# Slots ahead of the gates, table angles in VectorE's gaps, and table doublings with both parts in one instruction

## What is computed

```python
xn = layernorm(x)
# state space part: a long convolution per channel, whose kernel K has 1024 taps
V  = exp(dtA[:, :, None] * l[None, None, :])        # complex, 128 heads x 64 states x 1024 lags
K  = 2 * real(einsum('hn,hnl->hl', Ct, V))
y  = irfft(rfft(xn) * rfft(K))[:1024]
# experts part: 8 experts, each row goes to its best 2
gate_logits = einsum('bsd,ed->bse', xn, Wg)
gating = softmax over the two largest logits
out = sum over those two: gating * (silu(xn W1) * (xn W2)) W3
x = x + layernorm(...y...) + out
```

## Time and profile before

| | us |
|---|---|
| median of 3 runs | 861.29 |
| lowest and highest | 860.84 to 863.75 |
| span of the profiled execution | 820.2 |
| PE busy | 757.8 (92%) |
| DVE busy | 658.9 (80%) |
| ACT busy | 550.4 (67%) |
| POOL busy | 146.5 (18%) |

### The profile page before, as it was taken

One profiled execution on the slowest core, in us unless ns is written; L12 is line 12 of the kernel. 1 busy time (PEld: TensorE's weight loads), 2 busy tenths in 40 slices (PEclk: granted clock), 3 DMA queues, 4 the chain that ended last, 5 costly groups with the idle time before them and its releaser, 6 DMA issues.

```text
span 820.2 us, 11626 instructions
## 1 busy us (share of the span) xinstructions
PE 757.8 (92%) x3893; PEld 615.2 (75%) x3893; DVE 658.9 (80%) x1558; ACT 550.4 (67%) x939; POOL 146.5 (18%) x138
## 2 busy tenths in 40 slices
PE   6956366999999998999999999999999999999998
PEld 6624255888888645868788878887888887999997
DVE  7699767899937689998799889976777778877775
ACT  5833123344434368898999899889999997665663
POOL 0067775000000254643044000000000000000000
PEclk9978659899999999999999999999999999999999
DMA  8834582689876512413033112211211210000000
GB/s 251 347 104 137 185 285 90 200 250 289 291 223 195 163 40 70 86 54 89 15 102 81 40 38 59 47 43 44 55 45 49 52 27 0 14 14 20 14 20 27
DMA packets 81274, 85.15 MB, mean 104 GB/s; under 512 B 7361, under 2 KB 59841, under 8 KB 80961
## 3 DMA queue, kind: packets, MB, share of 16 engines
q1 hardware_dynamic: 77120, 76.04, 31.3%
q0 software_dynamic: 4096, 8.40, 3.5%
HBM read 59.12 MB, written 25.30 MB: 103 GB/s over the span
## 4 chain that ended last, share of the span: by engine, by line
PE 75%; POOL 9%; DVE 8%; issue 4%; ACT 3%; DMA 1%; SPq 0%; DVEq 0%; POOLq 0%
PE ps L1829 19%; PE ps L1831 18%; PE ps L1830 18%; POOL x_slots L643 9%; PE ps L1948 6%; PE ps L2024 3%; PE ps L2171 3%; DVE hid_lo L1755 2%; PE ps L1842 1%; PE ps L1927 1%; PE ps L2198 1%; PE ps L1869 1%; PE ps L1848 1%; DVE xn L1436 1%; ACT L880 1%
## 5 line engine op out<-in xcount | busy, mean ns | idle before, releaser
L1755 DVE TENSOR_TENSOR hid_lo<-hid,hid_hi 128x512 fp32r<-128x512 f32 x256 | 175.3, 686 | 52.1 <-ACT hid_hi L881 49.5
L880 ACT ACTIVATE hid<-ps,b_sb 128x512 f32<-128x512 f32 x256 | 177.7, 694 | 36.7 <-PE ps L1831 18.8
L881 ACT ACTIVATE hid_hi<-ps,b_sb 128x512 fp32r<-128x512 f32 x256 | 176.0, 688 | 0.0
L1829 PE MATMUL ps<-hid_hi,w_lo 128*128 128x512 f32 x256 | 102.1, 399 | 5.4 <-DVE hid_lo L1755 5.2
L1829 PE MATMUL ps<-xt_hi,w_lo 128*128 128x512 f32 x256 | 102.4, 400 | 1.5 <-DVE xn L1428 1.5
L1831 PE MATMUL ps<-xt_hi,w_hi 128*128 128x512 f32 x256 | 99.9, 390 | 0.0
L1831 PE MATMUL ps<-hid_hi,w_hi 128*128 128x512 f32 x256 | 99.8, 390 | 0.0
L1830 PE MATMUL ps<-xt_lo,w_hi 128*128 128x512 f32 x256 | 99.8, 390 | 0.0
L1830 PE MATMUL ps<-hid_lo,w_hi 128*128 128x512 f32 x256 | 99.8, 390 | 0.0
L792 ACT ACTIVATE act<-ps 128x512 f32<-128x512 f32 (+1 forms) x57 | 34.0, 596 | 81.6 <-PE ps L1831 81.6
L643 POOL DMA_INDIRECT x_slots<-xn,slot x64 | 71.4, 1115 | 62.6 <-DVE expert_of L1158 43.4
(11 more groups left out here) (337 smaller groups left out, 1543.9 us busy)
## 6 DMA issues: line engine op xcount, KB each, us to landing
gate_row<-gates_dram SPq DMA_DIRECT2D x64, 256.0 KB, 4.8
wc<-w_split SPq DMA_DIRECT2D x57, 256.0 KB, 3.7
w_split<-wc SPq DMA_DIRECT2D x8, 768.0 KB, 4.1
x_slots<-prod SPq DMA_DIRECT2D x11, 512.0 KB, 9.7
xc<-x_slots SPq DMA_DIRECT2D x19, 256.0 KB, 4.3
y_slots<-yo SPq DMA_DIRECT2D x19, 256.0 KB, 4.1
wst<-w SPq DMA_DIRECT2D x16, 256.0 KB, 4.7
wd<-w SPq DMA_DIRECT2D x19, 192.0 KB, 3.1
```

What stands on the lines that cost most here:

```text
L880: nc.scalar.activation(hid1[:, u % 4], ps[:, u % 4], ACT.Gelu_apprx_tanh, bias=b1_sb[:, u:u + 1])
L881: nc.scalar.activation(hid1_hi[:, u % 4], ps[:, u % 4], ACT.Gelu_apprx_tanh, bias=b1_sb[:, u:u + 1]).then_inc(hid1_done, 1)
L1755: tt(hid1_lo[:, u % 4], hid1[:, u % 4], hid1_hi[:, u % 4].bitcast(F32), sub).then_inc(hid1_lo_done, 1)
L1829: mm(dst, a_lo, b_hi, start=first, stop=False)
```

## The change

1. GpSimd's first scatter waits for `slots_done` 1 in place of 3.
2. VectorE no longer waits for ScalarE's exponential of the gates ahead of the slots: the wait and the four gate instructions move behind `doublings(1)`, and on ScalarE the exponential moves behind the copies of the spectra.
3. `angles()` is split. Its first three products go ahead of the second `scale0`, its other five instructions (`angles_rest`) go between the second one-hot and the slots, where `discretise()` stood; `discretise()` goes behind the slots. The imaginary parts of the `high` table turn the other way now, by a second row of lags with a sign (`turn_lags`).
4. ScalarE takes the exponential, the sines and the square of the base angles early, ahead of the third spectrum copy.
5. `doublings` handles real and imaginary part in one instruction: two multiplications and one sum for each table and step, twice as wide, with a product from a 4-dimensional view (row 4 of `base` is the sine with its sign changed twice, row 6 its negative) and a sum that reads the second factor backwards. `base_powers` has one instruction more.
6. `place` goes ahead of `doublings(0)`, and ScalarE copies the weights of experts 4 to 7 a step later (behind `k_copy(1)` and `k_copy(3)`), and waits for all eight low parts ahead of the copies of the taps' transform.

```diff
             pool.wait_ge(blanks_out, 16 * (-(-NC // 2) + 1))
-            pool.wait_ge(slots_done, 3)
+            pool.wait_ge(slots_done, 1)
...
             nc.scalar.activation(ks[:, 6], ks[:, 4], ACT.Exp).then_inc(trig_done, 1)
+            act_e.wait_ge(decay_done, 2)
+            nc.scalar.activation(base[:, 3], base[:, 3], ACT.Exp).then_inc(base_done, 1)
...
             for g in range(6, G):
                 normalise0(g)
-            act_e.wait_ge(top2_done, 1)
-            nc.scalar.activation(p2, m2, ACT.Exp).then_inc(top2_exp_done, 1)
+            act_e.wait_ge(phase_done, 2)
+            nc.scalar.activation(base[:, 4], base[:, 0], ACT.Sin, scale=TWO_PI).then_inc(base_done, 1)
+            nc.scalar.activation(base[:, 5], base[:, 0], ACT.Sin, scale=TWO_PI / 2).then_inc(base_done, 1)
+            act_e.wait_ge(base_done, 3)
+            nc.scalar.activation(base[:, 5], base[:, 5], ACT.Square).then_inc(base_done, 1)
             for n in range(2, 6):
                 spectrum_copy(n)
...
                 k_copy(c)
-                if c < 2:
-                    for e in range(2 * c + 4, 2 * c + 6):
+                if c % 2:
+                    for e in range(c + 3, c + 5):
                         w0_high(e)
...
             expm1_rest()
+            dve.wait_ge(route_in, 32)
+            angles()
             scale0(1)
...
             tt(member, oh1, oh2, add).then_inc(member_done, 1)
             tt(m2, m2, m1, sub).then_inc(top2_done, 1)
-            discretise()
-            dve.wait_ge(top2_exp_done, 1)
-            v = step.mark(ts(p1, p2, 1.0, None, add))
-            need(v)
-            v = step.mark(nc.vector.reciprocal(p1, p1))
-            need(v)
-            step.mark(tt(gate2[:], p2, p1, mul))
-            step.mark(nc.vector.tensor_copy(xn[:, :, P], p1))
+            angles_rest()
...
+            discretise()
             discretise_rest()
...
                 for n in range(5):
...
-                        step.mark(tt(tmp_(0), re[:, :, a], c, mul))
-                        step.mark(tt(tmp_(1), im[:, :, a], s, mul))
-                        step.mark(tt(tmp_(2), re[:, :, a], s, mul))
-                        v_low = step.mark(tt(tmp_(3), im[:, :, a], c, mul))
...
-                        step.mark(tt(re[:, :, b_], tmp_(0), tmp_(1), sub))
-                        step.mark(tt(im[:, :, b_], tmp_(2), tmp_(3), add))
...
+                    for table, lag_, at in tables:
+                        here = table[:, :, hs, a]
+                        cosine = base[:, 5, lag_ + n, hs].unsqueeze(1).unsqueeze(3).broadcast_to((P, 2, HC, 1 << n))
+                        sines = base[:, 4:7:2, lag_ + n, hs].unsqueeze(3).broadcast_to((P, 2, HC, 1 << n))
+                        step.mark(tt(half_way[:, at:at + 2, :, a], here, cosine, mul))
+                        ready.append(step.mark(tt(half_way[:, at + 2:at + 4, :, a], here, sines, mul)))
+                    for (table, lag_, at), v in zip(tables, ready):
                         need(v)
+                        crossed = half_way[:, at + 3:at + 1:-1, :, a]
+                        op = tt(table[:, :, hs, b_], half_way[:, at:at + 2, :, a], crossed, add)
...
             w0_low(0)
             w0_low(1)
             base_powers()
+            dve.wait_ge(ident_done, 1)
+            v = step.mark(nc.vector.memset(place[:], 0.0))
+            need(v)
+            nc.vector.reduce_sum(place[:, 3 * LO:4 * LO], ident.rearrange("p (a n) -> p n a", a=HG), AX.X).then_inc(place_done, 1)
             doublings(0)
             w0_low(2)
             w0_low(3)
             doublings(1)
+            dve.wait_ge(top2_exp_done, 1)
```

More of the change, by code:

```diff
@@ L1072, in discretise_rest, with angles, angles_rest @@
                 v = step.mark(ts(K(21), K(19), -1.0, None, mul))
+            FH, FL, AR, CTR, CTI = K(15), K(16), K(4), K(19), K(22)
+            def angles():
+                k = lambda i: base[:, i]
+                col = lambda a: a.unsqueeze(1).broadcast_to((P, NB, HH))
+                lag, turn = (a.unsqueeze(2).broadcast_to((P, NB, HH)) for a in (base_lags, turn_lags))
+                tt(k(3), col(AR), lag, mul).then_inc(decay_done, 1)
+                step.mark(tt(k(0), col(FH), turn, mul))
+                step.mark(tt(k(2), col(FL), turn, mul))
+            def angles_rest():
+                k = lambda i: base[:, i]
+                need(step.n)
+                v1 = step.mark(ts(k(1), k(0), MAGIC, MAGIC, add, sub))
+                need(v1)
+                v1 = step.mark(tt(k(0), k(0), k(1), sub))
+                need(v1)
+                v1 = step.mark(tt(k(0), k(0), k(2), add))
+                need(v1)
+                v1 = step.mark(ts(k(1), k(0), MAGIC, MAGIC, add, sub))
+                need(v1)
+                tt(k(0), k(0), k(1), sub).then_inc(phase_done, 1)
             expm1_start()
@@ L1203, in base_powers @@
                 v1 = step.mark(ts(k(1), k(5), -2.0, 1.0, mul, add))
-                step.mark(tt(k(6), k(3), k(4), mul))
+                v2 = step.mark(tt(k(4), k(3), k(4), mul))
                 need(v1)
-                v1 = step.mark(tt(k(5), k(3), k(1), mul))
-                need(v1)
+                step.mark(tt(k(5), k(3), k(1), mul))
+                need(v2)
+                v2 = step.mark(ts(k(6), k(4), -1.0, None, mul))
+                need(v2)
             def doublings(d):
                 hs = slice(d * HC, (d + 1) * HC)
-                re, im, g0, g1 = low[:, 0, hs], low[:, 1, hs], high[:, 0, hs], high[:, 1, hs]
+                tables = ((low, 0, 0), (high, NB // 2, 4))
@@ L1213, in doublings @@
+                step.mark(nc.vector.memset(low[:, 0, hs, 0:1], 1.0))
+                step.mark(nc.vector.memset(low[:, 1, hs, 0:1], 0.0))
+                step.mark(nc.vector.tensor_copy(high[:, 0, hs, 0:1], CTR[:, hs].unsqueeze(2)))
+                v = step.mark(ts(high[:, 1, hs, 0:1], CTI[:, hs].unsqueeze(2), -1.0, None, mul))
                 for n in range(5):
                     a, b_ = slice(0, 1 << n), slice(1 << n, 2 << n)
-                    wide_ = lambda i, v: base[:, v, i, hs].unsqueeze(2).broadcast_to((P, HC, 1 << n))
@@ L1240, in doublings @@
-                    need(v_high)
-                    v = step.mark(tt(g0[:, :, b_], tmp_(4), tmp_(5), add))
-                    if n < 4:
-                        v = step.mark(tt(g1[:, :, b_], tmp_(6), tmp_(7), sub))
-                        need(v)
-                    else:
-                        need(v)
-                        tt(g1[:, :, b_], tmp_(6), tmp_(7), sub).then_inc(tables_done, 1)
-            angles()
+                    need(v)
+                    ready = []
+                    for table, lag_, at in tables:
[4 more added lines that the diff above has]
+                        ready.append(step.mark(tt(half_way[:, at + 2:at + 4, :, a], here, sines, mul)))
@@ L1250, in _ @@
+                    for (table, lag_, at), v in zip(tables, ready):
+                        need(v)
+                        crossed = half_way[:, at + 3:at + 1:-1, :, a]
+                        op = tt(table[:, :, hs, b_], half_way[:, at:at + 2, :, a], crossed, add)
+                        if table is high and n == 4:
+                            op.then_inc(tables_done, 1)
+                        else:
+                            v = step.mark(op)
             w0_low(0)
@@ L1256, in _ @@
             doublings(1)
+            dve.wait_ge(top2_exp_done, 1)
+            v = step.mark(ts(p1, p2, 1.0, None, add))
+            need(v)
+            v = step.mark(nc.vector.reciprocal(p1, p1))
+            need(v)
+            step.mark(tt(gate2[:], p2, p1, mul))
+            step.mark(nc.vector.tensor_copy(xn[:, :, P], p1))
             for e in range(4, E):
@@ L2258, in layout @@
             .reshape(E, J0, P, P).transpose(0, 2, 1, 3).reshape(E, P, J0 * P)], 2),
[L2259 removed]
+        lag_row=np.concatenate([np.arange(LO), lags, np.where(np.arange(NB) < NB // 2, lags, -lags), E - np.arange(E), np.tril(np.ones((E, E))).ravel()]).astype(np.float32),
         prefix=prefix.reshape(2, P, T * E + E).transpose(1, 0, 2),
```

61 lines of the change are left out of this document (9 added, 52 removed).

## The result

The changed kernel takes 842.05 us (median of 4 runs, 839.15 to 843.42) against 861.15 for the one before (4 runs, 860.84 to 863.75): a ratio of 0.9741, interval 0.9703 to 0.9779, so 2.6% faster. The prediction had 860.1, with 855.0 to 862.8 as its range.

What follows compares the result with a forecast made beforehand. Bound: the end of GpSimd's 64 scatters and what follows up to chunk 1's first matmul, then TensorE. Head start -4.3, scatter waits +4.8, behind the last scatter -1.66: -1.2 us, giving 860.1; range 855.0 to 862.8.

Steps and rivals of the forecast that it cites:

- First scatter: GpSimd's head start: slots 3.30 us earlier and release 1.06 us earlier, sum 4.3 us, first scatter at 41.6 instead of 45.95.
- second tables: VectorE's tables for TensorE: ready at about 86 instead of 95.83, sum -10 us.
- the products ahead of `scale0`: Three VectorE products of `angles` taking 2.2 us, covered by waits for ScalarE and TensorE: no cost; 2.2 without these covers.
- rivals on slower patterns: VectorE's 4-dimensional and backward patterns run slower, waits grow about 4 to 5 us more: 864.6 us; chance 0.07.
- a missing head start: Something else holds GpSimd's first scatter, blank rows or last normalised tile: 864.4 us; chance 0.02.
- The contention: Scatters' waits beside VectorE instructions grow by 4.8 us; scatter mean near 1.19 instead of 1.115, last scatter at 136.1.
- the prediction's own sign: The prediction is wrong if, among other signs, the mean of GpSimd's scatters stays at 1.1 us or less.
- rival 1: GpSimd's head start arrives whole or nearly so, scatter waits hardly growing: 857.1 or 855.3 us; chance 0.30.
- The execution of the profile is taken to stand for the median 861.29: In the sum: -1.2 us in the profile's 820.2 span carried over to the median, time around the span unchanged: 860.1.
- 15 us of the tables' path turn into slack: Ahead of chunk 0: taps ready near 113, but chunk 0 waits for rows SyncE asked for at 119.60.
- chunk 0 near 121: TensorE starts chunk 0 at about 121 instead of 128.60, the taps' turning starting at 92.
- The term of 1.66 us: Behind the last scatter: VectorE's products done by about 138, so its low part of chunk 1 starts 1.66 us earlier.

Runs made afterwards that it cites:

- experiments 2 and 8: Changed kernel, first scatter waiting for slots_done 3 again: 840.49 us; kernel before with part 1 alone, first scatter after slots_done 1: 862.55 us.
- before_again: The kernel before, unchanged, traced again: median 862.78 us; the traced execution 868.15 us with a span of 866.3.
- vector_delay: Kernel before with 8 idle memsets of 128x512 on VectorE ahead of doublings(0): 873.39 us, ratio 1.0071.
- before_wait1: Kernel before with part 1 alone, first scatter after slots_done 1: 862.55 us, ratio 0.998.
- low_later: Kernel before with w0_low(1), two VectorE instructions, moved from ahead of base_powers() to behind doublings(0): 870.62 us, ratio 1.0133.
- tensor_padding: Kernel before with 20 idle products on TensorE behind the spectra 3 to 8: 860.42 us, ratio 0.995.
- place_early: Kernel before with part 6 alone: 864.82 us.
- after_delay: Changed kernel with 12 idle memsets of 128x512 on VectorE ahead of doublings(0): 849.14 us, ratio 0.9854.
- new_doublings: Kernel before with part 5 alone, both parts of the doublings in one instruction: 849.43 us, ratio 0.9822.
- old_doublings: Changed kernel with the doublings, base powers and lags of before: 847.18 us.
- after_delay_long: Changed kernel with 20 idle memsets of 128x512 on VectorE ahead of doublings(0): 845.02 us, ratio 0.9818.
- late_place: Changed kernel with part 6 taken back: 847.42 us, ratio 0.9836.
- experiments 3 and 5: Changed kernel with the doublings, base powers and lags of before: 847.18 us; kernel before with part 5 alone: 849.43 us.
- 7: Kernel before with the new doublings and 50 one-column memsets between their steps on VectorE: 849.18 us.
- 9: Idle VectorE memsets of 128x512 ahead of doublings(0): 8 in the kernel before, 873.39 us; 12 and 20 in the changed kernel, 849.14 and 845.02 us.
- 11: 20 idle TensorE products: before 860.42, changed 840.0 us; 32 TensorE semaphore increments: before 861.63 us; 64 on SyncE: changed 841.94 us.
- the 32 increments: Kernel before with 32 increments of an unused semaphore on TensorE ahead of its wait for the one-hots: 861.63 us, ratio 1.0002.

## Why the prediction was wrong

**What was right.** First scatter at 41.82 (41.6 predicted); a wide instruction 1.14 from start to start (1.15) and the wait beside it 1.96 - 0.95 = 1.01 (1.04); second tables at 86.3 (86); next to no cost for the products ahead of `scale0` (the second one-hot at 33.94 in place of 33.74). The rivals on slower patterns and on a missing head start did not come about. The contention was over-sized: the mean of the scatters is 1.098 us, not 1.19, since VectorE does nothing from 111.4 to 136.45 and the scatters there take 0.96. (By the prediction's own sign, a mean of 1.1 or less, it was wrong here.) The last one starts at 131.29 in place of 136.1. That is rival 1 as far as the scatters go, but it is not what made the time: experiments 2 and 8 move the scatters by 1 us and find nothing.

**The step that failed** is the one in the sum: "The execution of the profile is taken to stand for the median 861.29 with what lies around the span unchanged". 41.1 us beside a span of 820.2 should have been asked for a reason; it was the sign that this execution lacked some 40 us that the timed ones take. From it followed the second wrong step: "15 us of the tables' path turn into slack". In the shown execution the chain from the tables to the taps' transform is ahead of the scatters and gains nothing by being earlier. In those like `before_again` it is the path that sets the end: chunk 0 is turned at 163.49 there, and in the changed kernel at 137.68.

Even against the shown execution the forecast does not hold: it had chunk 0 near 121, with TensorE's turning of the taps at 92 and SyncE's requests as early as before. The turning began at 98.65, the requests came at 135.70 in place of 119.60, and chunk 0 at 137.68. That is 17 of the 20 us between the span forecast, 819.0, and the measured 839.2. The term of 1.66 us failed with it: the product steps could not be done by 138, VectorE took chunk 1's low part at 154.43 behind them, and chunk 1's first product began at 155.22 in place of 143.3, for another reason than the last scatter. A slip in the sum of the scatters (63 periods of 1.26 us are 79.4, not 79.5) changes nothing.

**What stands in its place.** In executions with pauses, TensorE, ScalarE, VectorE and SyncE can each be held while the scatters run, and what is then not done is done behind 133 to 138. The time follows how far TensorE's chain has come by then. From the traces (us; the second tables are ready at the end of VectorE's last instruction for them, "taps turned" is the start of line 1907; the last two columns are the time of the execution traced and the median of the runs):

| kernel | second tables | L1896 ends | taps turned | transform ends | chunk 0 turned | traced | median |
|---|---|---|---|---|---|---|---|
| before, as shown | 95.8 | 101.2 | 108.2 | 127.9 | 128.6 | | |
| vector_delay | 144.7 | 151.3 | 156.4 | 176.0 | 176.7 | 877.23 | 873.39 |
| before_wait1 | 130.3 | 142.6 | 143.8 | 163.0 | 163.7 | 862.16 | 862.55 |
| before_again | 102.9 | 142.4 | 143.6 | 162.8 | 163.5 | 868.15 | 862.78 |
| low_later | 125.1 | 140.9 | 141.9 | 162.4 | 163.1 | 867.79 | 870.62 |
| tensor_padding | 96.7 | 124.7 | 141.9 | 161.1 | 161.8 | 864.79 | 860.42 |
| place_early | 98.3 | 123.1 | 139.5 | 159.0 | 159.7 | 863.28 | 864.82 |
| after_delay | 94.3 | 101.1 | 109.1 | 148.9 | 149.6 | 854.41 | 849.14 |
| new_doublings | 92.5 | 99.0 | 104.7 | 147.2 | 147.9 | 851.64 | 849.43 |
| old_doublings | 88.8 | 95.4 | 109.6 | 144.1 | 144.8 | 846.14 | 847.18 |
| after_delay_long | 100.5 | 106.9 | 110.1 | 134.5 | 139.9 | 842.77 | 845.02 |
| late_place | 84.7 | 90.2 | 97.6 | 137.7 | 139.5 | 842.81 | 847.42 |
| after | 86.4 | 91.7 | 98.7 | 118.4 | 137.7 | 841.00 | 842.05 |

Above are the kernels whose taps are turned only when the scatters are over, whether line 1896 or VectorE was what kept them (chunk 0 from 159.7 on); in the middle those whose taps are turned before and transformed late (139.5 to 149.6); and last the changed one, where all of it is through by 118.4 and ScalarE and SyncE are what is held. From chunk 0's turning to the end of the span it is 696.7 to 703.8 us in all the profiled executions of all kernels but the shown one. So the gain (25.8 of 27.1 us in the pair of traces, 19 in the medians) is that more of TensorE's chain gets through in the scatters' stretch. Either of the two halves alone already gets the taps turned before the end of the scatters (experiments 3 and 5), which is why they do not add up.

Why the change gets it through is not shown. It moves the tables up by 10 us by its own rows (parts 3, 4 and 5), but that is not what decides: `after_delay_long` has its tables at 100.5 and is not held in line 1896, `tensor_padding` has them at 96.7 and is.

**What stays open.** Why TensorE or VectorE is held at the tables in all but one trace of the kernel before with the old doublings, and in none with the new ones. (`old_doublings`, the changed kernel without them, stands between: short pauses in its first products, none in its second.) So the shape of the new doublings is the rival that is left, and no run takes it apart. It is not the number of VectorE's instructions (7), not when the line starts (9), not the first scatter's time (2, 8), and not the place in TensorE's stream alone (11). Nor do the runs tell what hands out the instructions every 0.7 us. The queue whose packets the profile lists as "instruction" had one of 16 KB near the place where the pauses begin: 0.93 us long at 82.3 in the shown execution of before, 2.01 at 81.9 in `before_again`. That a slow packet is the cause is not borne out: it took 0.93 at 83.2 in `before_wait1`, where the pauses had begun at 82.7, and 1.45 at 82.8 in `low_later`, where TensorE ran through. With the 20 products it came at 66.3 and the pauses of the first products were gone, with the 32 increments at 78.4 and they were not. No run took such a packet away from the scatters. The Trainium skill (Runtime: NRT & Kernel Launch, Instruction fetch mechanics) calls the cost of coming to a new block mostly hidden; no run here shows that this is what costs, and none that it isn't. As every execution compared here was recorded, no run tells either whether recording has a part in the pauses.

The Trainium skill (SBUF — State Buffer, Who interferes with whom) says that a tensor_tensor was not seen to stall the DMAs that GpSimd issues. The traces say otherwise, 0.54 us beside one of 512 elements and 1.01 beside one of 1024; the measurement decides, and the forecast's use of it was right.

## What to carry to other kernels

Before a profile is used for a sum, compare its own time with the timed runs; a gap that the ends of the span can't hold (here 41 us where the other traces have 1.7 to 2.0) means that the profile shows another execution than the one that is timed, and slack read from it need not be slack. While GpSimd issues indirect DMAs back to back, other engines' short instructions can come at a fraction of their pace, so look in the trace for starts a multiple of some 0.7 us apart and ask how much of the next stage's chain gets through before the DMAs end. Changes of such a chain need not add up: here they paid when another piece of it got through, and a chain that started later could still get through.

## What the runs showed of the hardware

- While the 64 scatters ran, 64 semaphore increments on SyncE took 10.8 and 11.8 us in place of 4.3, in portions 0.70 to 0.75 us apart; TensorE got one product of the tables per 0.7 to 2.8 us over 34 us (102.97 to 137.21), and ran on at full pace from 137.91, 4.6 us after the end of the scatters' last packet.
- Not every execution has it: in the shown one of before SyncE issued 35 short instructions from 110.45 to 117.35 at full pace beside the scatters.
- Executions of one program differ in time: part 6 alone took 834.51 once and 863.28 to 868.90 three times; the kernel before has a span of 820.2 in one execution and 866.3 in another.
- A scatter that starts just inside a VectorE instruction of 1024 elements with two inputs from SBUF takes 1.96 us, inside one of 512 1.50, alone 0.96.
- VectorE's 4-dimensional and backward patterns cost nothing extra: 1.14 us per 1024 elements from start to start, against 0.60 per 512.
